# Cross-attention and FFN kernel: the two fp16 parts of a half of the probabilities turned by one transposing transfer instead of two

## The chip, the cores and the metric

The kernel runs on one core of one Trainium2 chip. The metric is the device time of one execution in microseconds (us). Engines are named as in the profile: PE is TensorE (PEld its weight loads), DVE is VectorE, ACT is ScalarE, POOL is GpSimd, and SP is SyncE, whose queue (SPq) issues nearly all the DMAs.

## What is computed

The inputs are `x` of 32 x 128 x 1024 and a context of 32 x 128 x 256, in float32. The reference, cut to what matters:

```python
def _layernorm(x):                      # over the last axis, eps 1e-5
    ...
def _L0_xattn_ref(pcd_up, pcd_down, Wq, Wk, Wv, Wskip):
    q = jnp.einsum('oc,bcn->bon', Wq, pcd_up)
    k = jnp.einsum('oc,bcm->bom', Wk, pcd_down)
    v = jnp.einsum('oc,bcm->bom', Wv, pcd_down)
    energy = jnp.einsum('bcn,bcm->bnm', q, k) / sqrt(C)
    attention = jax.nn.softmax(energy, axis=-1)
    return jnp.einsum('oc,bcn->bon', Wskip, pcd_up) + jnp.einsum('bnm,bcm->bcn', attention, v)
def _L0_ffn_ref(x, qweight, scales, zeros, bias):
    w = dequantised 4-bit weights, 1024 x 1024
    return jnp.einsum('bsi,io->bso', x, w) + bias
x = x + _L0_xattn_ref(_layernorm(x), ctx_1024, ...)
x = x + _L0_ffn_ref(_layernorm(x), ...)
```

## The kernel before, in words

One batch element b (128 channels by 1024 positions) is one unit of work; there are 32. The kernel is a software pipeline written out by hand: every engine has a function `step(t)`, and in step t it works on several elements at once: on n = t + 1 (centring, keys and values), b = t (scores and softmax), a = t - 1 (attention output, residual, second norm), q = t - 2 (the FFN) and c = t - 3 (output). There is no planner: each engine runs its calls in the order in which they are written, and semaphores tie the engines together. The first two steps have an order of their own (`run_in`).

Precision is held by splitting each float32 operand into a high and a low part. The probabilities of an element (1024 positions by 256 context columns) lie as 128 x 2048 in `prob`. They are handled in two halves h = 0 and 1 of 512 positions:

- POOL scales them by the inverse row sums (`normalise`, line 259), in four chunks j.
- ACT rounds a half to fp16, the high part (`probs_hi`, line 483, 128 x 1024 elements into `p_hi`).
- DVE takes the difference, the low part (`probs_lo`, line 662, into `p_lo`).
- SP turns both with transposing DMAs (`turn_probs`): line 166 for the high part once it is made, line 169 for the low part once that is made. Each moves 128 x 1024 fp16 elements from SBUF to SBUF. Both add 16 to `pt_loaded[h]`.
- PE waits for both (line 911) and multiplies with the values (`skip_attend`, line 914).

PE attends to half 0 of element a early in step t = a + 1 and to half 1 later in it. ACT writes `p_hi` of the next element only after the transfers of the last one have landed (line 482), and the new softmax overwrites `prob` only after the low part is made (line 472).

The normalised residual stream is turned in the same way: ACT makes `xn` and its high part (lines 492 and 501), POOL the low part (line 301), SP turns both (`turn_xn`, lines 177 and 183), and PE's `ffn` waits for both landings and runs 32 matmuls over them (line 919), with a closing matmul that adds the zero-point and bias terms (line 923).

SP's queue is strictly in order. In step t it issues: the two halves of an output (line 198), the next context and the next `x` (lines 147 and 144), `turn_probs(b, 0)`, `turn_probs(b, 1)`, `turn_xn(a)` and the three small copies of the row sums (line 189). Whatever one of these waits for, and however long its issue takes, holds up the ones behind it:

```python
if ran(b):
    turn_probs(b, 0)
    turn_probs(b, 1)
if ran(a):
    turn_xn(a)
```

The other places that the steps below touch: POOL computes the inverse standard deviation of the second norm (line 283) from DVE's variance (line 687), and from it the bias (line 285) that ACT needs for `xn`. DVE reads the maximum of the context from PSUM (line 615) as soon as PE's keys and values are done (line 897), adds the residual (line 672) and scales the FFN product (line 696).

Of the kernel before, what the change touches and what calls it, by code (L numbers as in the profile page):

```python
# [7 lines left out]
F16 = mybir.dt.float16  # L8
# [6 lines left out]
def xattn_ffn_program(nc, x, ctx_in, wq, wk, wv, wskip, qweight, scales, zeros, bias, out):  # L15
# [5 lines left out]
    P = nc.NUM_PARTITIONS  # L21
    HALF = 512
    HALVES = N // HALF
    NT = N // P
    MT = M // P
# [15 lines left out]
    with es:  # L41
        def sb(name, shape, dt=F32):
            return es.enter_context(nc.sbuf_tensor("sb_" + name, shape, dt))

        def pb(name, shape, dt=F32):
            return es.enter_context(nc.psum_tensor("ps_" + name, shape, dt))
# [4 lines left out]
        def sems(name, n):  # L51
            return [sem(f"{name}{k}") for k in range(n)]
# [30 lines left out]
        neg_max = sb("neg_max", [P, CHUNKS, TPC])  # L83
        esum = sb("esum", [P, CHUNKS, TPC])
        rsum = sb("rsum", [P, CHUNKS, TPC])
        p_hi, p_lo = (sb(n, [P, HALVES, MT, HALF], F16) for n in ("p_hi", "p_lo"))
        pt_hi, pt_lo = (sb(n, [P, HALVES, MT, HALF], F16) for n in ("pt_hi", "pt_lo"))
        x1 = sb("x1", [P, 3, N])
        xn = sb("xn", [P, KT, P])
        xn_hi, xn_lo = (sb(n, [P, KT, P], F16) for n in ("xn_hi", "xn_lo"))  # L90
        xnt_hi, xnt_lo = (sb(n, [P, 2, KT, P], F16) for n in ("xnt_hi", "xnt_lo"))
# [8 lines left out]
        ps_o = [pb(f"o{k}", [P, HALF]) for k in range(HALVES)]  # L100
# [19 lines left out]
        phi_done, plo_done, pt_loaded = sems("phi", HALVES), sems("plo", HALVES), sems("pt_loaded", HALVES)  # L120
# [8 lines left out]
        def ran(b, back=0):  # L129
            return 0 <= b - back < B  # L130
# [4 lines left out]
        def run_steps(step, first):  # L135
            for t in range(first, B + 3):
                step(t)
# [3 lines left out]
        @block.sync  # L141
        def _(sp):
            def load_x(k):
                sp.dma_start(x_sb[:, k % 4, :], x[k, :, :]).then_inc(x_loaded[k % 4], 16)

            def load_ctx(k):
                sp.dma_start(ctx_sb[:, k % 2, :], ctx_in[k, :, :]).then_inc(ctx_loaded[k % 2], 16)

            load_x(0)
            load_ctx(0)  # L150
            for dst, src in ((wv_sb, wv), (wskip_sb, wskip)):
                sp.dma_start(dst[:, :], src).then_inc(wvs_loaded, 16)
            q_tiles = qweight.rearrange("(t p) o -> p t o", p=P)
            load_x(1)
            load_ctx(1)
            for t in range(QT):
                sp.dma_start(q_sb[:, t, :], q_tiles[:, t, :]).then_inc(q_loaded[t], 16)
                if t == 1:
                    load_x(2)
            sp.dma_start(scale_row[:, :], scales.broadcast_to((P, OUT))).then_inc(row_loaded, 16)  # L160

            def turn_probs(b, h):
                sp.wait_ge(phi_done[h], b + 1)
                if ran(b, 1):
                    sp.wait_ge(attn_done[h], b)
                sp.dma_start_transpose(pt_hi[:, h, :, :].rearrange("m k (t n) -> m (k t) n", n=P),
                                       p_hi[:, h, :, :].rearrange("n k m -> n (k m)")).then_inc(pt_loaded[h], 16)
                sp.wait_ge(plo_done[h], b + 1)
                sp.dma_start_transpose(pt_lo[:, h, :, :].rearrange("m k (t n) -> m (k t) n", n=P),  # L169
                                       p_lo[:, h, :, :].rearrange("n k m -> n (k m)")).then_inc(pt_loaded[h], 16)  # L170

            def turn_xn(a):
                par = a % 2
                sp.wait_ge(xnhi_done, a + 1)
                if ran(a, 2):
                    sp.wait_ge(y_done[1], a - 1)
                sp.dma_start_transpose(xnt_hi[:, par, :, :],  # L177
                                       xn_hi[:, :, :].rearrange("c k r -> c (k r)")).then_inc(
                    last_hi_loaded if a == B - 1 else xnt_loaded[par], 16)
                sp.wait_ge(xnlo_done, a + 1)  # L180
                if a == B - 1:
                    sp.wait_ge(last_lo_done, 1)
                sp.dma_start_transpose(xnt_lo[:, par, :, :],
                                       xn_lo[:, :, :].rearrange("c k r -> c (k r)")).then_inc(xnt_loaded[par], 16)
                sp.wait_ge(rs3_done, a + 1)
                if a == 0:
                    sp.wait_ge(seed_made, 3)
                for k, row in ((0, 0), (1, 1), (0, 32)):
                    sp.dma_start(seed_l[row:row + 1, par, :].bitcast(F32),
                                 rs3[:, par, k:k + 1].bitcast(F32)).then_inc(rs_loaded[par], 16)  # L190

            def step(t):
                b, a, c = t, t - 1, t - 3
                if ran(c):
                    for h in range(HALVES):
                        cols = slice(h * HALF, (h + 1) * HALF)
                        sp.wait_ge(out_done[h], c + 1)
                        sp.dma_start(out[c, :, cols], o_sb[:, c % 2, cols]).then_inc(stored[c % 2], 16)
                if ran(t + 3):
                    sp.wait_ge(kv_done, t + 2)  # L200
                    load_ctx(t + 3)
                    sp.wait_ge(x1_done[1], a + 1)
                    load_x(t + 3)
# [6 lines that stand above are left out]
            def run_in():  # L210
                sp.wait_ge(kv_done, 1)
                load_ctx(2)
                load_x(3)
                turn_probs(0, 0)
                turn_probs(0, 1)
                sp.wait_ge(kv_done, 2)
                load_ctx(3)
                turn_probs(1, 0)
                sp.wait_ge(kv_done, 3)
                load_ctx(4)  # L220
                sp.wait_ge(x1_done[1], 1)
                load_x(4)
                turn_probs(1, 1)
                turn_xn(0)

            run_in()
            run_steps(step, 2)
            for par in range(2):
                sp.wait_ge(stored[par], 32 * (B // 2))
# [183 lines left out]
        def _(act):  # L413
# [64 lines left out]
            def probs_hi(b, h):  # L478
                act.wait_ge(norm_done[2 * h], b + 1)
                act.wait_ge(norm_done[2 * h + 1], b + 1)  # L480
                if ran(b, 1):
                    act.wait_ge(pt_loaded[h], 32 * b)
                act.activation(p_hi[:, h, :, :].rearrange("n k (t m) -> n k t m", m=P),  # L483
                               prob[:, 2 * h:2 * h + 2, :, :].rearrange("n j t (k m) -> n k (j t) m", m=P),
                               ACT.Copy).then_inc(phi_done[h], 1)

# [22 lines left out]
            def run_in():  # L509
# [8 lines left out]
                centred_hi(1)  # L518
                exps(0, 2)
                probs_hi(0, 0)  # L520
                exps(0, 3)
                keys_hi(1)
# [50 lines left out]
        def _(dve):  # L573
# [85 lines left out]

            def probs_lo(b, h):  # L660
                dve.wait_ge(phi_done[h], b + 1)
                dve.tensor_tensor(p_lo[:, h, :, :].rearrange("n k (t m) -> n k t m", m=P),  # L662
                                  prob[:, 2 * h:2 * h + 2, :, :].rearrange("n j t (k m) -> n k (j t) m", m=P),
                                  p_hi[:, h, :, :].rearrange("n k (t m) -> n k t m", m=P),
                                  ALU.subtract).then_inc(plo_done[h], 1)

            def residual(a, h):
# [185 lines left out]
        def _(pe):  # L853
            HI_LO = ((0, 0), (0, 1), (1, 0))
            wsk_p, xc_p, k_p, v_p = (wsk_hi, wsk_lo), (xc_hi, xc_lo), (k_hi, k_lo), (v_hi, v_lo)
            pt_p, xnt_p = (pt_hi, pt_lo), (xnt_hi, xnt_lo)

            pe.wait_ge(wkq_loaded, 32)
            pe.matmul(ps_o[0][:, 0:C], wk_sb[:, :], wq_sb[:, :], start=True, stop=True).then_inc(key_done, 1)
# [45 lines left out]
            def skip_attend(a, h):  # L905
                cols = slice(h * HALF, (h + 1) * HALF)
                if ran(a, 1):
                    pe.wait_ge(x1_done[h], a)
                for i, (s, m) in enumerate(HI_LO):
                    pe.matmul(ps_o[h][:, :], wsk_p[s][:, a % 3, :], xc_p[m][:, a % 3, cols], start=i == 0, stop=False)  # L910
                pe.wait_ge(pt_loaded[h], 32 * (a + 1))
                for k in range(MT):
                    for i, (s, m) in enumerate(HI_LO):
                        last = pe.matmul(ps_o[h][:, :], v_p[s][:, a % 3, k * P:(k + 1) * P], pt_p[m][:, h, k, :],  # L914
                                         start=False, stop=k == MT - 1 and i == 2)
                last.then_inc(attn_done[h], 1)

# [120 lines left out]
```

## Time and profile before

| | |
|---|---|
| runs of the kernel before | 530.37, 531.56 and 531.84 us, median 531.56 us |
| the profiled execution's own time | 532.22 us |
| its span, first to last instruction | 530.4 us |
| mean granted TensorE clock | 0.987 of full speed |

The profiled execution is one more run, 0.66 us above the median of the three. Durations below come from it. A line of a timeline gives the start (us from the start of the span) and the duration of an instruction or of a merged group (xN), then engine, line, operation and operands. A wait is idle time of an engine, put down to what ended it.

### The profile page before, as it was taken

How to read it: one execution, taken by the hardware profiler on the slowest of the kernel's cores; microseconds unless marked ns; L12 is line 12 of the kernel's file. 1: busy time of each engine (PE TensorE's matmuls, PEld its weight loads, DVE VectorE, ACT ScalarE, POOL GpSimd, SP SyncE). 2: the span in 40 equal slices, each digit the busy share in tenths (PEclk: the TensorE clock that was granted, in tenths of full speed). 3: DMA queues.
4: the chain of work that ended last, by engine and by line, in shares of the span. 5: the costliest groups of instructions: out<-in, count | busy, mean ns of one | idle time of the engine just before them, and what ended most of it. 6: DMA issues, size and time to landing. Idle time of an engine off the chain costs nothing.

```text
span 530.4 us, 9275 instructions
## 1 busy us (share of the span) xinstructions
PE 504.5 (95%) x2700; PEld 311.9 (59%) x2700; DVE 441.2 (83%) x982; ACT 369.7 (70%) x844; POOL 435.0 (82%) x649
## 2 busy tenths in 40 slices
PE   4659899999999999999999999999999999999987
PEld 3546565566666565666656566665656666565643
DVE  5899788899888889988888998888889888887752
ACT  4878876767787776777777677777767777777520
POOL 4888788898888889888888988888898888888753
PEclk9788999999999999999999999999999999999999
DMA  8727877788898799789888978987797889758864
GB/s 294 192 61 129 159 191 180 176 187 181 172 168 194 178 176 195 178 167 166 197 178 177 191 161 189 162 200 178 176 179 179 182 160 201 179 128 150 155 127 116
DMA packets 236787, 91.65 MB, mean 173 GB/s; under 512 B 219200, under 2 KB 223808, under 8 KB 236736
## 3 DMA queue, kind: packets, MB, share of 16 engines
q1 hardware_dynamic: 236016, 90.92, 79.8%
q8 instruction: 21, 0.34, 0.3%
q14 instruction: 30, 0.25, 0.2%
q10 hardware_dynamic: 720, 0.14, 0.1%
HBM read 23.87 MB, written 16.78 MB: 77 GB/s over the span
## 4 chain that ended last, share of the span: by engine, by line
POOL 63%; issue 14%; ACT 7%; PE 3%; DVE 1%; DMA 1%; SPq 1%; POOLq 0%; ACTq 0%
POOL sb_prob L259 13%; POOL sb_xc_lo L274 13%; POOL sb_xn_lo L301 13%; POOL sb_o L253 12%; ACT sb_xn L492 6%; POOL sb_nb L285 4%; POOL sb_rstd L283 3%; PE ps_y L919 3%; POOL sb_rstd L267 3%; POOL sb_rs L293 1%; POOL sb_rs L295 1%; DMA sb_xnt_lo<-sb_xn_lo 1%; ACT sb_xn_hi L501 0%; SPq L169 0%; SPq L177 0%
## 5 line engine op out<-in xcount | busy, mean ns | idle before, releaser
L919 PE MATMUL ps_y<-sb_wf,sb_xnt_hi 128*128 128x512 f16 x512 | 192.3, 380 | 3.6 <-ACT sb_wf L506 1.9
L919 PE MATMUL ps_y<-sb_wf,sb_xnt_lo 128*128 128x512 f16 x512 | 191.8, 379 | 0.0
L474 ACT ACTIVATE sb_prob<-ps_e,sb_neg_max 128x256 f32<-128x256 f32 x256 | 118.0, 469 | 35.8 <-DVE sb_neg_max L653 35.7
L259 POOL TENSOR_SCALAR sb_prob<-sb_prob,sb_rsum 128x256 f32<-128x256 f32 x256 | 123.2, 497 | 4.1 <-DVE sb_rsum L658 4.1
L662 DVE TENSOR_TENSOR sb_p_lo<-sb_prob,sb_p_hi 128x1024 f16<-128x1024 f32 x64 | 78.1, 1220 | 49.3 <-ACT sb_p_hi L483 49.3
L301 POOL TENSOR_TENSOR sb_xn_lo<-sb_xn,sb_xn_hi 128x512 f16<-128x512 f32 x63 | 75.2, 1214 | 44.2 <-ACT sb_xn_hi L501 44.2
L483 ACT ACTIVATE sb_p_hi<-sb_prob 128x1024 f16<-128x1024 f32 x64 | 67.3, 1051 | 51.4 <-issue 47.5
L884 PE MATMUL ps_e<-sb_k_hi,sb_xc_hi 128*128 128x256 f32 x256 | 85.1, 332 | 10.3 <-DVE sb_k_lo L641 5.5
L919 PEld LDWEIGHTS ps_y<-sb_wf,sb_xnt_hi 128*128 128x128 f16 x512 | 49.9, 98 | 67.7 <-issue 8.3
L653 DVE TENSOR_REDUCE sb_neg_max<-ps_e 128x2 f32<-128x512 f32 x128 | 84.6, 679 | 1.3 <-PE ps_e L884 1.2
L253 POOL TENSOR_TENSOR sb_o<-sb_prod,sb_x 128x512 f32<-128x512 f32 x63 | 80.3, 1295 | 5.4 <-DVE sb_prod L696 5.4
L919 PEld LDWEIGHTS ps_y<-sb_wf,sb_xnt_lo 128*128 128x128 f16 x512 | 50.1, 98 | 53.0 <-issue 0.5
L274 POOL TENSOR_TENSOR sb_xc_lo<-sb_xc,sb_xc_hi 128x512 fp32r<-128x512 f32 x62 | 80.4, 1296 | 0.0
L492 ACT ACTIVATE sb_xn<-sb_x,sb_nb,sb_rstd 128x1024 f32<-128x1024 f32 x32 | 42.9, 1340 | 51.4 <-POOL sb_nb L285 51.4
L884 PE MATMUL ps_e<-sb_k_lo,sb_xc_hi 128*128 128x256 f32 x256 | 73.6, 287 | 0.0
L884 PE MATMUL ps_e<-sb_k_hi,sb_xc_lo 128*128 128x256 f32 x256 | 73.5, 287 | 0.0
L884 PEld LDWEIGHTS ps_e<-sb_k_hi,sb_xc_hi 128*128 128x128 f32 x256 | 49.9, 195 | 20.2 <-DVE sb_k_lo L641 11.2
L696 DVE TENSOR_TENSOR sb_prod<-ps_y,sb_scale_row 128x512 f32<-128x512 f32 x64 | 43.6, 681 | 11.5 <-PE ps_y L923 11.5
L884 PEld LDWEIGHTS ps_e<-sb_k_lo,sb_xc_hi 128*128 128x128 f32 x256 | 50.0, 195 | 2.7
L474 ACT ACTIVATION_READ_ACCUMULATOR sb_prob<-ps_e,sb_neg_max 128x1 f32 x256 | 51.0, 199 | 0.0
L672 DVE SCALAR_TENSOR_TENSOR sb_x<-ps_o,sb_o_scale,sb_x 128x512 f32<-128x512 f32 x64 | 47.2, 738 | 3.8 <-PE ps_o L914 3.8
L914 PE MATMUL ps_o<-sb_pt_hi,sb_v_hi 128*128 128x512 f16 x128 | 49.7, 388 | 0.7 <-DMA sb_pt_lo<-sb_p_lo 0.7
(115 smaller groups left out, 936.9 us busy)
## 6 DMA issues: line engine op xcount, KB each, us to landing
sb_x<-in_x_dram SPq DMA_DIRECT2D x32, 512.0 KB, 4.2
out_dram<-sb_o SPq DMA_DIRECT2D x64, 256.0 KB, 2.5
sb_ctx<-in_ctx_dram SPq DMA_DIRECT2D x32, 128.0 KB, 2.9
sb_q<-in_L_ffn_qweight_dram SPq DMA_DIRECT2D x4, 512.0 KB, 9.7
sb_seed_l<-sb_rs SPq DMA_DIRECT2D x96, 0.5 KB, 2.2
sb_pt_hi<-sb_p_hi SPq DMA_TRANSPOSE x64, 4.2
sb_pt_lo<-sb_p_lo SPq DMA_TRANSPOSE x64, 3.4
sb_scale_row<-in_L_ffn_scales_dram SPq DMA_DIRECT2D x1, 512.0 KB, 10.7
```

The lines of the kernel that those rows point to most:

```text
L253: pool.tensor_tensor(o_sb[:, c % 2, cols], prod[:, h, :], x1[:, c % 3, cols], ALU.add).then_inc(out_done[h], 1)
L259: last = pool.tensor_scalar(prob[:, j, t, :], prob[:, j, t, :], rsum[:, j, t:t + 1], P_SCALE, ALU.mult, ALU.mult)
L274: last = pool.tensor_tensor(xc_lo[:, n % 3, cols], xc[:, cols], xc_hi[:, n % 3, cols].bitcast(F32), ALU.subtract)
L301: last = pool.tensor_tensor(xn_lo[:, k:k + KT // 2, :], xn[:, k:k + KT // 2, :], xn_hi[:, k:k + KT // 2, :], ALU.subtract)
L474: done = act.activation(prob[:, j, t, :], ps_e[j % 2][:, t, :], ACT.Exp, bias=neg_max[:, j, t:t + 1], accum_out=esum[:, j, t:t + 1])
L483: act.activation(p_hi[:, h, :, :].rearrange("n k (t m) -> n k t m", m=P), prob[:, 2 * h:2 * h + 2, :, :].rearrange("n j t (k m) -> n k (j ...
L492: act.activation(xn[:, :, :].rearrange("c (t e) r -> c t e r", e=2), x1[:, a % 3, :].rearrange("c (t r e) -> c t e r", e=2, r=P), ACT.Iden ...
L653: dve.tensor_reduce(neg_max[:, j, :], ps_e[j % 2][:, :, :], AX.X, ALU.max, negate=True).then_inc(max_done[j], 1)
L662: dve.tensor_tensor(p_lo[:, h, :, :].rearrange("n k (t m) -> n k t m", m=P), prob[:, 2 * h:2 * h + 2, :, :].rearrange("n j t (k m) -> n k ...
L884: last = pe.matmul(ps_e[j % 2][:, t, :], xc_p[s][:, b % 3, cols], k_p[m][:, b % 2, :], start=i == 0, stop=i == 2)
L914: last = pe.matmul(ps_o[h][:, :], v_p[s][:, a % 3, k * P:(k + 1) * P], pt_p[m][:, h, k, :], start=False, stop=k == MT - 1 and i == 2)
L919: pe.matmul(ps_y[h][:, :], xnt_p[s][:, q % 2, kt, :], wf[:, kt, h * HALF:(h + 1) * HALF], start=kt == 0 and s == 0, stop=False)
```

## The change

The four tiles `p_hi`, `p_lo`, `pt_hi` and `pt_lo` become two, `p_parts` and `pt_parts`, in which the high part (index 0) and the low part (index 1) of each half lie side by side in a partition. `probs_hi` and `probs_lo` write into their part of `p_parts`. `turn_probs` waits for both parts, and then issues one transposing transfer of 128 x 2048 elements where there were two of 128 x 1024. A half's semaphore `pt_loaded[h]` therefore grows by 16 for each element instead of 32, and the waits for it are changed to match. The bytes moved, the instructions of ACT and DVE and the matmuls stay as they are.

```diff
-        p_hi, p_lo = (sb(n, [P, HALVES, MT, HALF], F16) for n in ("p_hi", "p_lo"))
-        pt_hi, pt_lo = (sb(n, [P, HALVES, MT, HALF], F16) for n in ("pt_hi", "pt_lo"))
+        p_parts = sb("p_parts", [P, HALVES, 2, MT, HALF], F16)
+        pt_parts = sb("pt_parts", [P, HALVES, 2, MT, HALF], F16)
...
                 sp.wait_ge(phi_done[h], b + 1)
                 if ran(b, 1):
                     sp.wait_ge(attn_done[h], b)
-                sp.dma_start_transpose(pt_hi[:, h, :, :].rearrange("m k (t n) -> m (k t) n", n=P),
-                                       p_hi[:, h, :, :].rearrange("n k m -> n (k m)")).then_inc(pt_loaded[h], 16)
                 sp.wait_ge(plo_done[h], b + 1)
-                sp.dma_start_transpose(pt_lo[:, h, :, :].rearrange("m k (t n) -> m (k t) n", n=P),
-                                       p_lo[:, h, :, :].rearrange("n k m -> n (k m)")).then_inc(pt_loaded[h], 16)
+                sp.dma_start_transpose(pt_parts[:, h, :, :, :].rearrange("m s k (t n) -> m (s k t) n", n=P),
+                                       p_parts[:, h, :, :, :].rearrange("n s k m -> n (s k m)")).then_inc(pt_loaded[h], 16)
...
                 if ran(b, 1):
-                    act.wait_ge(pt_loaded[h], 32 * b)
-                act.activation(p_hi[:, h, :, :].rearrange("n k (t m) -> n k t m", m=P),
+                    act.wait_ge(pt_loaded[h], 16 * b)
+                act.activation(p_parts[:, h, 0, :, :].rearrange("n k (t m) -> n k t m", m=P),
...
-                dve.tensor_tensor(p_lo[:, h, :, :].rearrange("n k (t m) -> n k t m", m=P),
+                dve.tensor_tensor(p_parts[:, h, 1, :, :].rearrange("n k (t m) -> n k t m", m=P),
...
-                pe.wait_ge(pt_loaded[h], 32 * (a + 1))
+                pe.wait_ge(pt_loaded[h], 16 * (a + 1))
                 for k in range(MT):
                     for i, (s, m) in enumerate(HI_LO):
-                        last = pe.matmul(ps_o[h][:, :], v_p[s][:, a % 3, k * P:(k + 1) * P], pt_p[m][:, h, k, :],
+                        last = pe.matmul(ps_o[h][:, :], v_p[s][:, a % 3, k * P:(k + 1) * P], pt_parts[:, h, m, k, :],
```

## Rows read from the trace of the kernel before

**Rows 1.** The page, part 1: busy time of each engine.
```profile
PE 504.5 (95%) x2700; PEld 311.9 (59%) x2700; DVE 441.2 (83%) x982; ACT 369.7 (70%) x844; POOL 435.0 (82%) x649
```

**Rows 2.** The page, part 4: the chain that ended last, by engine.
```profile
POOL 63%; issue 14%; ACT 7%; PE 3%; DVE 1%; DMA 1%; SPq 1%; POOLq 0%; ACTq 0%
```

**Rows 3.** Timeline of POOL over one step: start, duration, line.
```profile
260.33 2.38 POOL L301 TENSOR_TENSOR sb_xn_lo<-sb_xn,sb_xn_hi 128x512 f16<-128x512 f32 x2 [1.44 <-ACT sb_xn_hi L501]
...
270.93 0.56 POOL L283 TENSOR_TENSOR sb_rstd<-sb_ve,sb_neg_half 128x1 f32<-128x1 f32 x1
...
275.77 2.38 POOL L301 TENSOR_TENSOR sb_xn_lo<-sb_xn,sb_xn_hi 128x512 f16<-128x512 f32 x2 [1.44 <-ACT sb_xn_hi L501]
```

**Rows 4.** Timeline of PE around two steps, the instructions that wait for DMAs.
```profile
251.99 0.39 PE L919 MATMUL ps_y<-sb_wf,sb_xnt_hi 128*128 128x512 f16 x1
...
260.75 0.61 PE L897 MATMUL ps_kv<-sb_proj,sb_ctx 128*128 128x128 f32 x4
...
261.89 0.39 PE L914 MATMUL ps_o<-sb_pt_hi,sb_v_hi 128*128 128x512 f16 x1
...
265.33 0.39 PE L914 MATMUL ps_o<-sb_pt_hi,sb_v_hi 128*128 128x512 f16 x1
...
267.36 0.39 PE L919 MATMUL ps_y<-sb_wf,sb_xnt_hi 128*128 128x512 f16 x1
```

**Rows 5.** Waits of PE's weight loads, 100 to 500 us: total us, times, longest.
```profile
PEld ps_y L919 <- DMA sb_xnt_lo<-sb_xn_lo: 1.2, 4, 0.5
PEld ps_o L914 <- DMA sb_pt_lo<-sb_p_lo: 1.0, 2, 0.7
```

**Rows 6.** Timeline of SP's queue, 248 to 270 us: start and duration of each issue.
```profile
248.66 1.36 SPq L183 DMA_TRANSPOSE sb_xnt_lo<-sb_xn_lo  x1
...
256.79 1.23 SPq L169 DMA_TRANSPOSE sb_pt_lo<-sb_p_lo  x1
259.33 1.23 SPq L166 DMA_TRANSPOSE sb_pt_hi<-sb_p_hi  x1
260.60 1.34 SPq L169 DMA_TRANSPOSE sb_pt_lo<-sb_p_lo  x1
262.04 1.28 SPq L177 DMA_TRANSPOSE sb_xnt_hi<-sb_xn_hi  x1
263.36 1.34 SPq L183 DMA_TRANSPOSE sb_xnt_lo<-sb_xn_lo  x1
264.75 1.89 SPq L189 DMA_DIRECT2D sb_seed_l<-sb_rs  x3
266.68 1.06 SPq L198 DMA_DIRECT2D out_dram<-sb_o  x2
```

**Rows 7.** Four transfers by line, windows 247:255, 256:258, 260:262, 262:275: issue to landing.
```profile
L183 SPq DMA_TRANSPOSE sb_xnt_lo<-sb_xn_lo x1: 1363/1363/1363, 248.7 to 248.7; - x1
...
DMA to landing us min/median/max: 3.3/3.3/3.3
...
L169 SPq DMA_TRANSPOSE sb_pt_lo<-sb_p_lo x1: 1233/1233/1233, 256.8 to 256.8; - x1
...
DMA to landing us min/median/max: 3.1/3.1/3.1
...
L169 SPq DMA_TRANSPOSE sb_pt_lo<-sb_p_lo x1: 1336/1336/1336, 260.6 to 260.6; - x1
...
DMA to landing us min/median/max: 3.4/3.4/3.4
...
L183 SPq DMA_TRANSPOSE sb_xnt_lo<-sb_xn_lo x1: 1342/1342/1342, 263.4 to 263.4; - x1
...
DMA to landing us min/median/max: 3.2/3.2/3.2
```

**Rows 8.** Short windows: busy time of each engine, then clock, DMA share and GB/s.
```profile
259.50:260.45 0.95, 0.95 (x10) 0.95 (x9) 0.95 (x1) 0.95 (x2) 0.12 (x1) 1.00 0.00 0
260.50:261.90 1.40, 1.40 (x10) 1.03 (x9) 1.36 (x5) 0.89 (x2) 1.40 (x2) 1.00 0.99 189
...
267.10:267.70 0.60, 0.60 (x6) 0.41 (x5) 0.60 (x1) 0.14 (x2) 0.60 (x1) 1.00 0.13 1
267.80:268.80 1.00, 1.00 (x6) 0.49 (x5) 1.00 (x4) 0.00 (x0) 1.00 (x3) 1.00 1.01 373
```

**Rows 9.** Timeline of DVE in the same step: the instructions tied to PE and POOL.
```profile
261.68 0.15 DVE L615 TENSOR_SCALAR sb_t_scale<-ps_m 128x1 f32<-128x1 f32 x1
...
270.62 0.15 DVE L687 TENSOR_SCALAR sb_ve<-sb_mv 128x1 f32<-128x1 f32 x1
```

**Rows 10.** The chain that ended last, in order of time, 504 to 515 us.
```profile
504.09 1.24 DVE sb_p_lo L662
505.32 0.04 issue
505.36 1.39 SPq L169
...
506.85 1.28 SPq L177
508.13 0.04 issue
508.18 3.20 DMA sb_xnt_lo<-sb_xn_lo
511.38 0.05 issue
511.43 3.63 PE ps_y L919 x16
```

More of the change, by code:

```diff
@@ L661, in probs_lo @@
                 dve.wait_ge(phi_done[h], b + 1)
-                dve.tensor_tensor(p_lo[:, h, :, :].rearrange("n k (t m) -> n k t m", m=P),
+                dve.tensor_tensor(p_parts[:, h, 1, :, :].rearrange("n k (t m) -> n k t m", m=P),
                                   prob[:, 2 * h:2 * h + 2, :, :].rearrange("n j t (k m) -> n k (j t) m", m=P),
-                                  p_hi[:, h, :, :].rearrange("n k (t m) -> n k t m", m=P),
+                                  p_parts[:, h, 0, :, :].rearrange("n k (t m) -> n k t m", m=P),
                                   ALU.subtract).then_inc(plo_done[h], 1)
@@ L855, in _ @@
             wsk_p, xc_p, k_p, v_p = (wsk_hi, wsk_lo), (xc_hi, xc_lo), (k_hi, k_lo), (v_hi, v_lo)
-            pt_p, xnt_p = (pt_hi, pt_lo), (xnt_hi, xnt_lo)
+            xnt_p = (xnt_hi, xnt_lo)
             pe.wait_ge(wkq_loaded, 32)
```

## The prediction, made before the changed kernel was run

> **What bounds the kernel now.** I read the page first, then the chain that ended last, the waits of each engine, and a timeline of one step. By busy time PE looks like the bound, at 95% [rows 1]. But the chain of work that ended last lies 63% on POOL and 3% on PE [rows 2]. The timeline tells how both can be. POOL's `xn_lo` of one step starts at 260.33 and of the next at 275.77, a period of 15.44 us, and POOL waits in it only for work that ACT does on POOL's own results [rows 3]. PE's first FFN matmul starts at 251.99 and again at 267.36, a period of 15.37 [rows 4]. So two loops run side by side, POOL's being 0.07 us a step slower. PE creeps forward against POOL until it meets a transfer that isn't there yet: in the 400 us from 100 to 500, some 26 steps, it waited 4 times for the turned `xn_lo` and 2 times for the turned `p_lo`, 2.2 us in all [rows 5]. These waits cost nothing today, since POOL sets the pace. What counts is how much later a landing may come before the delay travels through PE and DVE into POOL.
>
> **The slack of each landing.** For one ordinary step, issue [rows 6] plus issue to landing [rows 7] against the matmul that needs it [rows 4]:
> - Half 0: issued 256.79, + 3.1 = 259.9, needed 261.89, slack 2.0.
> - Half 1: 260.60 + 3.4 = 264.0, needed 265.33, slack 1.3.
> - `xn_lo`: 263.36 + 3.2 = 266.6, needed 267.36, slack 0.8.
> - `xn_lo` one step earlier, a late one: 248.66 + 3.3 = 251.96, needed 251.99, slack 0.03.
>
> Behind PE there is a little more. PE's keys and values end at 260.75 + 0.61 = 261.36 [rows 4] and DVE reads them at 261.68, 0.32 later; DVE's variance is ready at 270.77 [rows 9] and POOL takes it at 270.93 [rows 3], 0.16 later. Between the two I see DVE without idle time. So a landing of `xn_lo` may come later by 0.8 + 0.32 + 0.16 = 1.3 us in an ordinary step and by 0.03 + 0.48 = 0.5 in a late one. Anything beyond goes into POOL's loop, and so into the time.
>
> **The change, part by part.** *Removed:* 64 issues of 1.23 us on SP (line 166). *Kept:* the bytes; ACT's and DVE's instructions have the same shapes and counts, so I cost them at nothing. *Changed:* each half's transfer is now issued when the low part is made (256.79, 260.60), and is twice as long. The high part loses its head start of 2.5 us in half 0 and 1.3 in half 1.
>
> What a double transfer costs isn't in the trace. Bounds for its issue: not under one issue, 1.23 us; two issues back to back, 1.23 + 1.34 = 2.6 [rows 6]. I take 2.4, near the upper end, because the data side is as slow as the issue side: with the first transfer issued at 259.33, no byte moves from 259.50 to 260.45, and from 260.50 on the DMA engines are 0.99 busy at 189 GB/s [rows 8]. One part is 128 x 1024 x 2 = 0.26 MB, which at 189 to 211 GB/s is 1.2 to 1.4 us; a gap-free stream of two parts saves at most a tenth or two. (211 is 0.26 MB over one 1.24 us issue.)
>
> Does the stream start while the double transfer is still being issued? The plain DMAs of the outputs help: issue of two from 266.68 to 267.74, no data until 267.70, and 373 GB/s from 267.80 [rows 8]. There the data come 1.1 us after the first issue begins, and that issue takes about half of 1.06 us [rows 6], so data lag the end of an issue by some 0.5 us. For a transposing one they begin at its end or just before. So its first pieces must have been handed over half way through, and a double one should start to move at + 1.2 too. Its landing is then later than that of the second of two transfers by the time of one part less what overlapped.
>
> - Half 0: 3.1 + 1.2 = 4.3 us after 256.79, at 261.1; slack 2.0 goes to 0.8. Costs nothing; if late, it would be PE's first attention matmul.
> - Half 1: before, `p_lo` queued just behind `p_hi`. Now 260.60 + 3.4 + 1.0 = 265.0; slack 1.3 goes to 0.3. In the two waits for `p_lo` of rows 5 it goes under zero by 1.0, but PE's next FFN waits then anyway.
> - `turn_xn`, moved behind a longer issue: before, SP was free at 260.60 + 1.34 = 261.94, now at 260.60 + 2.4 = 263.0. The issues of lines 177 and 183 move from 262.04 and 263.36 to 263.05 and 264.4, so both land 1.0 us later, `xn_lo` at 267.6. PE now waits 0.2 to 0.3 us in an ordinary step.
> - Behind it on SP stand the three row-sum copies, the outputs, the next context and `x`, all + 1.0. The row sums were issued at 264.75, and their matmul comes after 16 FFN matmuls; I cost them at nothing, and if that cover went, line 923 would wait.
>
> **The sum.** An ordinary step has 1.3 us of slack against 1.0: nothing. A late step has 0.5 against 1.0: 0.5 us each. How many are late? Rows 5 record 6 waits in 26 steps; the one at 251.99 isn't among them as a long wait, and with such near misses I estimate 8 to 9, so 10 in the 30 steps that turn an `xn` behind probabilities. That gives 10 x 0.5 = 5.0 us. At the end there is no slack: the chain goes from DVE's last `p_lo` through SP's issue at 505.36 (1.39 us) and line 177 to the `xn_lo` transfer and the last FFNs [rows 10]; 1.0 us more. Sum: 6.0 us. On the profiled execution's own 532.22 that is 538.2; the median of the runs shown is 0.66 lower, so I say 537.6.
>
> The unknown is the lateness D of `xn_lo`, 1.0 here. With D = 0.5 late steps cost nothing, and the sum is 0.5; with D = 1.3 they cost 0.8 each, ordinary ones begin to count, and the sum is about 10.
>
> The trace has one part in 1.2 to 1.4 us. The Trainium skill (DMA: Bandwidth & Descriptors, "Latency and other measured facts") gives 261 GB/s for a transposing DMA as measured; by that an estimate for the double transfer is 2.0 us, D would be about 0.5, and the time 532.1. The same page's rule to coalesce transfers ("Rules for kernel authors") speaks for the change, but no transfer here is of the small kind that it means.
>
> **The rivals.**
> *A. Not slower: one long transfer streams better.* If the double issue takes no more than 1.34 + 0.5 = 1.84 us, `xn_lo` comes at most 0.5 late and the slack takes it. Time 532.1, within the noise. For it: every issue has some fixed part, and SP issues of plain DMAs take only some 0.5 us each. Against: the DMA engines are full while a part moves [rows 8], and a faster issue doesn't help a full engine. If even the single issue's length held, nothing would be gained beyond PE's idle waits, as POOL paces the loop.
> *B. Transfer only after the whole issue.* If data move only once all is issued, the first byte comes at + 2.4 instead of + 1.2, half 1 lands 1.2 later still, and `xn_lo` queues behind it: D = 2.1. Late steps then cost 2.1 - 0.5 = 1.6 each, ordinary ones 0.8, though the path from FFN back to the next but one `xn_lo` takes two steps, so about 5 of those count: 16 + 4 + 2 = 22 us, 554. For it: in rows 8 the data of a single transfer start about when its issue ends. Against: the half microsecond of lag in the plain DMAs.
> *C. The transfer is cut into two again by whatever expands it.* Then both parts are issued back to back after the low part, 2.6 us of issue, D = 1.1 to 1.2: 540. It is the upper end of my own case.
>
> **How the numbers follow.** A difference under 0.3% (1.6 us) can't be told from no change here. My forecast with C has 0.68, from 533.5 to 542; A 0.17; B 0.11; a remaining 0.04 for a gain that I have no mechanism for. Slower is 0.80, same 0.16 (most of A), faster 0.04. The range, 531 to 545, holds my case and A, with the late steps counted up to 14, and leaves out B and the gain.
>
> **What would show it.** Right: the issue of the merged transfer takes 2.2 to 2.6 us and lands 4.2 to 4.6 after it starts; SP's line for `xnt_lo` starts 1.0 later against POOL's step; PE's waits for `xnt_lo` grow from 1.2 us to 5 or more in the same window; POOL's wait for DVE's variance, absent now, appears in some steps; a few steps are longer than 15.44. Wrong: the issue under 1.9 us (A), landing over 5 us (B), or waits on PE that grow while POOL's period stays: then the slack behind PE was larger than the 0.48 I read.

## The result, and the profile after

The changed kernel takes 534.04 us (median of 6 runs, 533.51 to 535.31), the kernel before 531.46 (6 runs, 530.37 to 531.87). The ratio is 1.0052, with a 95% interval of 1.0038 to 1.0066: slower by 2.6 us, where I forecast 6.0. The direction is right, the time is inside the range, and the size is less than half of the forecast. The profiled execution has a span of 533.5 us, 3.1 more than before. It is the slowest of its six runs (535.31 us), so the 3.1 holds some scatter from run to run. The granted clock isn't the cause: it is 1.00 from 100 to 500 us in both traces.

The page of the changed kernel, parts 1 and 4, against [rows 1, 2]:

```profile
PE 504.7 (95%) x2700; PEld 311.8 (58%) x2700; DVE 430.4 (81%) x982; ACT 370.5 (69%) x844; POOL 435.0 (82%) x649
...
POOL 38%; PE 15%; issue 11%; DVE 10%; ACT 6%; DMA 6%; SPq 4%; POOLq 0%; ACTq 0%
```

POOL's share of the chain fell from 63% to 38%, and DMA, PE, DVE and SP came in: the chain now crosses from transfers into POOL in some steps. The other change is easily missed. DVE is busy 10.8 us less than before, with the same 982 instructions. Where that comes from is shown below; it is the key to the size of the loss.

SP's queue in an ordinary step, against [rows 6] (start, duration):

```profile
262.35 1.97 SPq L175 DMA_TRANSPOSE sb_xnt_hi<-sb_xn_hi  x1
264.37 1.33 SPq L181 DMA_TRANSPOSE sb_xnt_lo<-sb_xn_lo  x1
```

and the two merged transfers of the same step, by line, in windows 256:258 and 260:262, against [rows 7]:

```profile
L167 SPq DMA_TRANSPOSE sb_pt_parts<-sb_p_parts x1: 1808/1808/1808, 256.8 to 256.8; - x1
...
DMA to landing us min/median/max: 4.3/4.3/4.3
...
L167 SPq DMA_TRANSPOSE sb_pt_parts<-sb_p_parts x1: 1673/1673/1673, 260.6 to 260.6; - x1
...
DMA to landing us min/median/max: 4.3/4.3/4.3
```

The landing of the merged transfer came out as worked out, 4.3 us after its issue. Its issue did not: 1.7 to 1.8 us in this step (median of all 64: 1.9) instead of 2.4. Yet `xn_lo` is issued at 264.37 where it was 263.36, 1.0 us later, just as forecast. The time that the merged issue saved appears in the next one: line 175 now takes 1.97 us where line 177 took 1.28 [rows 6]. Two short windows of the same step (busy times of the engines, then clock, DMA share and GB/s) tell what the data did:

```profile
260.70:261.70 1.00, 1.00 (x9) 0.95 (x9) 0.98 (x2) 0.53 (x1) 1.00 (x2) 1.00 0.00 0
261.80:264.80 3.00, 3.00 (x20) 2.07 (x19) 2.48 (x11) 2.87 (x8) 3.00 (x3) 1.00 1.10 210
```

The merged transfer is issued at 260.58 and its issue lasts until 262.25, but data move from about 261.8 on, so it streams while it is issued. From there the DMA engines are full, at 210 GB/s, through the merged transfer and into the next one. Before, the stream was as full, but it began at 260.50 [rows 8], with the high part. So `xn` comes 1.0 us later because the stream starts that much later. That fits the DMA engines, and not the length of an issue on SP, as what sets the pace here; no run varied the length of an issue by itself.

PE's waits for DMAs between 100 and 500 us, against [rows 5], and POOL's waits for DVE in the same window (total us, times, longest):

```profile
PEld ps_o L912 <- DMA sb_pt_parts<-sb_p_parts: 3.4, 7, 0.9
PEld ps_y L917 <- DMA sb_xnt_lo<-sb_xn_lo: 2.4, 6, 0.6
POOL sb_prob L257 <- DVE sb_rsum L656: 1.9, 7, 0.5
```

PE's weight loads wait 5.8 us now against 2.2, and POOL, which never waited for DVE before in this window, does so 7 times. That is the new wait through which the loss enters POOL's loop. It stands at line 257 (`normalise`), for the inverse row sums, and not at the inverse standard deviation where I expected it.

**Where the 3.1 us of span come from.** I took the start of POOL's `xn_lo` for each element from the timelines of both kernels. Up to element 2 the changed kernel is 0.5 us ahead. That isn't an effect of the change: over the ten traces of this case this start lies anywhere from 73.6 to 75.4 us. From element 2 to element 28 (26 periods) the kernel before takes 401.6 us and the changed one 403.4: + 1.8. From there to the end it is 53.9 before and 55.6 after: + 1.7. Before, all 26 periods are 15.43 to 15.46 us. After, 21 are 15.40 to 15.50 us, and five are longer: 15.78, 15.76, 15.82, 16.36 and 15.78, which is 2.2 us above 15.45 in all; the ordinary periods, 0.02 to 0.03 shorter than before, give 0.4 back.

### The profile page after: what moved, and what is told of

It is laid out like the page before. It is cut to its first block, busy times and chain, and to the rows that moved or that the text cites. A ratio compares the mean times of both kernels' runs of the same rounds, so it can differ in the third digit from the quotient of the medians.

```text
span 533.5 us, 9213 instructions
## 1 busy us (share of the span) xinstructions
PE 504.7 (95%) x2700; PEld 311.8 (58%) x2700; DVE 430.4 (81%) x982; ACT 370.5 (69%) x844; POOL 435.0 (82%) x649
## 4 chain that ended last, share of the span: by engine, by line
POOL 38%; PE 15%; issue 11%; DVE 10%; ACT 6%; DMA 6%; SPq 4%; POOLq 0%; ACTq 0%
PE ps_y L917 11%; POOL sb_prob L257 8%; POOL sb_xc_lo L272 8%; POOL sb_xn_lo L299 8%; POOL sb_o L251 6%; ACT sb_xn L490 5%; DMA sb_xnt_lo<-sb_xn_lo 3%; POOL sb_nb L283 3%; DMA sb_pt_parts<-sb_p_parts 2%; POOL sb_rstd L281 2%; SPq L175 2%; SPq L167 2%; POOL sb_rstd L265 2%; DVE sb_p_parts L660 2%; DVE sb_x L670 1%
## 5 line engine op out<-in xcount | busy, mean ns | idle before, releaser
L660 DVE TENSOR_TENSOR sb_p_parts<-sb_prob,sb_p_parts 128x1024 f16<-128x1024 f32 x64 | 78.1, 1220 | 46.3 <-ACT sb_p_parts L481 46.3
L481 ACT ACTIVATE sb_p_parts<-sb_prob 128x1024 f16<-128x1024 f32 x64 | 67.2, 1050 | 30.2 <-issue 26.4
L912 PE MATMUL ps_o<-sb_pt_parts,sb_v_hi 128*128 128x512 f16 x256 | 76.9, 382 | 2.6 <-DMA sb_pt_parts<-sb_p_parts 2.6
```

Source lines behind the costliest of these rows:

```text
L481: act.activation(p_parts[:, h, 0, :, :].rearrange("n k (t m) -> n k t m", m=P), prob[:, 2 * h:2 * h + 2, :, :].rearrange("n j t (k m) -> n ...
L660: dve.tensor_tensor(p_parts[:, h, 1, :, :].rearrange("n k (t m) -> n k t m", m=P), prob[:, 2 * h:2 * h + 2, :, :].rearrange("n j t (k m) - ...
```

## The longest step, row by row

The period of 16.36 us is the one to read. SP's queue in it, from the changed kernel's timeline:

```profile
338.07 1.94 SPq L167 DMA_TRANSPOSE sb_pt_parts<-sb_p_parts  x1
340.10 2.49 SPq L175 DMA_TRANSPOSE sb_xnt_hi<-sb_xn_hi  x1
342.64 1.34 SPq L181 DMA_TRANSPOSE sb_xnt_lo<-sb_xn_lo  x1
```

PE and then DVE, from the same timeline (in brackets the idle time before an instruction and what ended it):

```profile
344.40 0.60 PE L912 MATMUL ps_o<-sb_pt_parts,sb_v_hi 128*128 128x512 f16 x2 [0.46 <-DMA sb_pt_parts<-sb_p_parts]
...
346.95 0.39 PE L917 MATMUL ps_y<-sb_wf,sb_xnt_hi 128*128 128x512 f16 x1 [0.37 <-DMA sb_xnt_lo<-sb_xn_lo]
...
354.55 0.69 DVE L694 TENSOR_TENSOR sb_prod<-ps_y,sb_scale_row 128x512 f32<-128x512 f32 x1 [1.06 <-PE ps_y L921]
...
356.36 0.16 DVE L613 TENSOR_SCALAR sb_t_scale<-ps_m 128x1 f32<-128x1 f32 x1 [0.41 <-PE ps_kv L895]
```

POOL, from one `xn_lo` to the next:

```profile
353.24 2.38 POOL L299 TENSOR_TENSOR sb_xn_lo<-sb_xn,sb_xn_hi 128x512 f16<-128x512 f32 x2 [1.44 <-ACT sb_xn_hi L499]
...
358.64 0.93 POOL L257 TENSOR_SCALAR sb_prob<-sb_prob,sb_rsum 128x256 f32<-128x256 f32 x2 [0.54 <-DVE sb_rsum L656]
...
362.52 0.93 POOL L257 TENSOR_SCALAR sb_prob<-sb_prob,sb_rsum 128x256 f32<-128x256 f32 x2 [0.22 <-DVE sb_rsum L656]
...
369.61 2.38 POOL L299 TENSOR_TENSOR sb_xn_lo<-sb_xn,sb_xn_hi 128x512 f16<-128x512 f32 x2 [1.45 <-ACT sb_xn_hi L499]
```

The merged transfer of half 1 is issued at 338.07 and lands 6.3 us later in place of 4.3 (its "DMA to landing"), PE waits for it and then for `xn_lo`, the FFN starts at 346.95, DVE waits 1.06 us for its product and 0.41 for the keys and values, and POOL waits 0.54 and 0.22 us for row sums. So both waits of PE, for half 1 and for `xn_lo`, stand in the same step; the last one is for `xn_lo`, which queues behind the merged transfer.

**Where the slack behind PE was.** DVE's instruction that makes the low part of the skip weights (`wsk_lo`, line 646 before, 644 after), grouped by line from 100 to 500 us: before, then after.

```profile
L646 DVE SCALAR_TENSOR_TENSOR sb_wsk_lo<-sb_proj,sb_sk_scale,sb_wsk_hi 128x128 fp32r<-128x128 f32 x25 | 29.0, 1162 | 0.0
```

```profile
L644 DVE SCALAR_TENSOR_TENSOR sb_wsk_lo<-sb_proj,sb_sk_scale,sb_wsk_hi 128x128 fp32r<-128x128 f32 x25 | 11.9, 476 | 0.0
```

The same instruction on the same shape takes 1162 ns in one kernel and 476 in the other. In the step shown next its start moved from 266.84 to 267.48, and its end hardly at all. Both ends lie 0.15 us behind the end of a POOL instruction with which it shares no data:

```profile
266.84 1.19 DVE L646 SCALAR_TENSOR_TENSOR sb_wsk_lo<-sb_proj,sb_sk_scale,sb_wsk_hi 128x128 fp32r<-128x128 f32 x1
...
266.59 1.29 POOL L274 TENSOR_TENSOR sb_xc_lo<-sb_xc,sb_xc_hi 128x512 fp32r<-128x512 f32 x1
```

```profile
267.48 0.46 DVE L644 SCALAR_TENSOR_TENSOR sb_wsk_lo<-sb_proj,sb_sk_scale,sb_wsk_hi 128x128 fp32r<-128x128 f32 x1
...
266.52 1.26 POOL L272 TENSOR_TENSOR sb_xc_lo<-sb_xc,sb_xc_hi 128x512 fp32r<-128x512 f32 x1
```

That isn't one step alone: in both kernels, and in the runs below that leave the instruction where it is, its end lies 0.14 to 0.15 us behind the end of a POOL instruction in most steps, while its duration has medians from 0.42 to 1.18 us. So most of the 1162 ns is a wait. The timeline counts this wait as busy time, with no releaser. DVE may start 0.7 us later and still finish at the same time. This is the slack that I missed: 0.32 + 0.16 = 0.48 us behind PE in the prediction, about 1.1 in fact.

## The experiments

**One half at a time.** `MERGED` names the halves that use the merged transfer; the other keeps two transfers, in the same tiles, and its semaphore counts 32.

```diff
+                if h in MERGED:
+                    sp.wait_ge(plo_done[h], b + 1)
+                    sp.dma_start_transpose(pt_parts[:, h, :, :, :]..., p_parts[:, h, :, :, :]...).then_inc(pt_loaded[h], 16)
+                    return
+                for s in range(2):
+                    if s == 1 or h in LATE:
+                        sp.wait_ge(plo_done[h], b + 1)
+                    sp.dma_start_transpose(pt_parts[:, h, s, :, :]..., p_parts[:, h, s, :, :]...).then_inc(pt_loaded[h], 16)
```

Half 0 alone:

> Only half 0 is merged; half 1 keeps its two transfers. Theory S (the cost sits in the late landings of half 1 and in the last steps, where xn_lo queues behind it): half 0 has 2.0 us of slack and loses 1.2, so nothing happens, the time is that of the kernel before within 0.3% (530.5 to 532.5), and PE's waits for the turned probabilities stay near 1.0 us between 100 and 500 us. Rival M (a merged transfer costs by itself, wherever it stands): about half of the loss, 532.5 to 533.

Measured: 531.31 us against 531.39, ratio 1.000 (0.999 to 1.0009). Half 0 costs nothing, and neither does the new layout of the tiles. PE's waits for probabilities were 1.6 us, not 1.0, and cost nothing either:

```profile
PEld ps_o L921 <- DMA sb_pt_parts<-sb_p_parts: 1.6, 4, 0.8
```

Half 1 alone:

> Only half 1 is merged. Theory S: nearly the whole loss of the full change, 533.5 to 534.3. Rival M: about half of it, 532.5 to 533. In both xn_lo is issued 1.0 to 1.1 us later against POOL's step.

Measured: 533.81 us, ratio 1.0042 (1.0026 to 1.0057), and `xn_lo` is issued 1.05 us later against POOL's step, as expected. Half 1 carries the loss. It is the half whose transfer stands directly ahead of those of `xn` on SP's queue.

**Two transfers, both issued late** (`MERGED` empty, `LATE` both halves):

> Two transfers in each half as before, but both are issued only once the low part is made. If the lost head start is the cost (theory S), this loses as much as the change or a little more: 533.5 to 535. If the length of one transfer is the cost (rival M), it is close to the kernel before: 531 to 532.5.

Measured: 536.42 us, ratio 1.010 (1.0084 to 1.0116): 5.0 us lost, more than expected, twice the loss of the change. So it is the lost head start that costs; once it is given up, one transfer is better than two. Against POOL's `xn_lo`, the low `xn` transfer lands at 6.4 us in the kernel before (median of the timelines' issues plus their landings), 7.5 with the merged transfer and 7.7 here. Only 0.25 us lie between the last two, but nine periods instead of five came out over 15.5 us.

**Only `xn` late.** The kernel before, with small DMAs put on SP's queue between the two kinds of transfer, in every step that has both. The probabilities are issued as before.

```diff
                 if ran(a):
+                    if ran(b):
+                        for k in range(2):
+                            sp.dma_start(spare[t:t + 1, k, :], wk_sb[0:1, :]).then_inc(spare_done, 16)
                     turn_xn(a)
```

> The kernel before with two small DMAs of 512 B put on SP's queue between the probabilities' transfers and those of xn, which start about 1.2 us later; the probabilities land as before. Theory of the prediction (slack behind PE is 0.48 us, late steps cost 0.5 each or more): 536 to 539. Theory S (DVE's step holds more slack, 0.7 us of it inside the 1.16 us instruction on line 646, so a late xn_lo is absorbed except at the end): 532 to 533.3, with POOL's period unchanged at 15.4 in nearly all steps.

Measured: 539.04 us, ratio 1.0142 (1.0125 to 1.0158), 7.6 us lost. At first sight this is my prediction's theory and not the new one. The trace says otherwise: POOL's 26 periods sum to only 2.7 us more than before, six of them over 15.5. The delay was also larger than planned, 1.65 us (median) instead of 1.2, since the queue stayed full from step to step; in about ten steps the low part of half 1 was issued later too, by 0.1 to 1.0 us. And 4.4 us were lost after element 28, where DVE makes the second half of the last `xn` low part only after it has scaled an FFN product, for which it waited 6.3 us here (the line below); SP can't issue that transfer before. So this end isn't comparable with the changed kernel's, and the run doesn't price a late `xn` by itself. The time lies outside the ranges of both theories. The run does show that a late `xn` alone produces POOL's new wait: from 100 to 500 us PE never waits for half 1, and POOL waits for DVE 9 times.

```profile
522.92 0.69 DVE L702 TENSOR_TENSOR sb_prod<-ps_y,sb_scale_row 128x512 f32<-128x512 f32 x1 [6.28 <-PE ps_y L929]
...
POOL sb_prob L265 <- DVE sb_rsum L664: 2.3, 9, 0.4
```

With one small DMA in place of two:

> The kernel before with one small DMA (0.6 us of SP's queue) ahead of the transfers of xn, in place of two. The law of a threshold (nothing until the FFN starts 8.1 to 8.2 us after POOL's xn_lo, then one for one): at most one or two steps longer than 15.5 us, and the loss is 0.5 to 1.5 us, most of it at the end: 532 to 533. A loss in proportion to the delay (half of the 7.6 us that two of them cost) gives 535.

Measured: 533.02 us against 531.27, ratio 1.0031 (1.0021 to 1.0042), just above what was expected. The `xn` transfer lands 0.7 us later than before, and only one period of the 26 is over 15.5 (15.52). In the trace the 26 periods take 0.7 us less than before and the end after element 28 takes 1.1 more, so this loss sits at the end. A delay of 0.7 costs 1.75 us, one of 1.65 costs 7.6 with the end in it: not in proportion.

**The law behind these runs.** I took it from the changed kernel and the first four runs; the one with a single small DMA and the three that follow the table were its tests. For each step I took the start of PE's first FFN matmul, counted from the start of POOL's `xn_lo` of the same element, and POOL's period that follows it. The latest ones, leaving out steps right after a longer one (there POOL has moved along already, and the same lateness costs nothing again):

| run | FFN start, us after `xn_lo` | POOL's period that follows |
|---|---|---|
| before | 7.57 | 15.44 |
| half 0 merged | 8.12 | 15.44 |
| one small DMA | 8.21 / 8.26 | 15.52 / 15.50 |
| changed kernel | 8.34 / 8.39 / 8.44 / 8.60 / 9.20 | 15.78 / 15.76 / 15.78 / 15.82 / 16.36 |
| half 1 merged | 8.26 / 8.58 | 15.54 / 15.81 |
| two transfers, both late | 8.63 / 8.93 / 9.05 | 15.86 / 16.17 / 16.29 |
| two small DMAs | 8.59 / 8.86 / 8.93 | 15.84 / 16.12 / 16.17 |
| `wsk_lo` moved, changed kernel | 8.54 / 8.70 | 15.56 / 15.72 |

Up to 8.1 or 8.2 us nothing happens, with one step as an exception (8.07 and 15.56 with half 1 merged; in the same step 15.50 and 15.51 in two other runs, which I can't explain); beyond it the period grows by roughly the excess. In the longest step above it is 346.95 - 337.75 = 9.20, and 16.36 - 15.45 = 0.91.

**The hidden wait taken out.** DVE's `wsk_lo` moved out of `values_lo` to a place just ahead of the second probabilities' low part, where DVE idles for ACT anyway and POOL waits too:

```diff
             def values_lo(n):
                 dve.wait_ge(kvhi_done, n + 1)
-                dve.scalar_tensor_tensor(wsk_lo[:, n % 3, :], ...)
+                if n < 3:
+                    skip_lo(n)
...
+                if ran(n):
+                    skip_lo(n)
                 if ran(b):
                     probs_lo(b, 1)
```

In the changed kernel:

> The changed kernel with DVE's low part of the skip weights (the 128 x 128 instruction that took 1.16 us before and 0.48 after) moved to the end of DVE's step, ahead of the second probabilities' low part, where DVE and POOL both wait for ACT. Theory R (that instruction holds a hidden wait for POOL, and with it the slack that took up most of the late transfers; steps grow only when the FFN's first matmul starts over 8.1 to 8.2 us after POOL's xn_lo): the instruction takes under 0.35 us in its new place, the threshold rises by the 0.4 us that it no longer takes in the chain, so the five longer steps shrink to one or two, and the time falls by 1 to 2 us, to 532 to 533; the loss at the end stays. If the slack was elsewhere: no change, 534.

Measured: 532.62 us against 531.27, ratio 1.0018 (1.0009 to 1.0027). How much of that is the slack is told by the same move in the kernel before, below. The instruction in its new place:

```profile
L643 DVE SCALAR_TENSOR_TENSOR sb_wsk_lo<-sb_proj,sb_sk_scale,sb_wsk_hi 128x128 fp32r<-128x128 f32 x26 | 8.9, 343 | 0.0
```

343 ns, as expected, and in most steps no POOL instruction runs beside it there; so 0.8 of the 1.16 us were waiting. The threshold rose (table: 8.54 gives 15.56, where 8.44 gave 15.78 before the move), though by less than the 0.4 us expected: after a late step the FFN's start settles at 8.35 us, where it settled at 8.09 in the changed kernel; and the longer periods shrank from 0.3 to 0.9 us over 15.45 to at most 0.3. There are four of them, where I expected one or two. The ordinary period fell as well, to 15.38, which is PE's own pace [rows 4].

In the kernel before:

> The kernel before with the same move. Theory R: no transfer is late enough to matter here, so only POOL's ordinary period can change, from 15.44 to about 15.41 us as in the changed kernel, where DVE's instruction did not wait: 530.3 to 531.4. If the move itself costs: above 532.

Measured: 531.05 us, ratio 0.9991 (0.9982 to 0.9999). The ordinary period is 15.39, 0.05 less. This is the run to hold the last one against, since the move shortens ordinary periods by itself: with the instruction moved in both, the change costs 1.6 us (532.62 against 531.05; 1.4 by the two ratios), where it costs 2.6 without the move. So a good two fifths of the loss are gone. The traces place the gain in the steps: from element 2 to 28 the change costs 0.6 us with the move (400.3 and 400.9) in place of 1.8, and after element 28 it costs 1.8 as before. That is what more slack behind PE should do, as the end has none. The move also takes the instruction itself out of the chain, so it doesn't price the hidden wait alone.

With half 0 merged too:

> Only half 0 merged, plus the same move: a candidate to beat both. Theory R: as the kernel before with the move, 530 to 531.3.

Measured: 530.89 us, ratio 0.9993 (0.9984 to 1.0002). Both are ahead of the changed kernel by 3 us, and by 0.2 and 0.4 us of the kernel before, which is less than a measurement of this kernel can tell.

## Why the prediction was right in sign and wrong in size

- *The reading of the bound* held: POOL's loop sets the pace, and a landing matters only when it gets through PE and DVE into it.
- *The cost of the double transfer* was right in its result and partly by luck. Landing after 4.3 us in both halves, and `xn_lo` issued 1.0 us later and landing at 267.6, are as forecast. But I derived the 1.0 from an issue of 2.4 us, and the issue took 1.7 to 1.8 here; what came 1.0 later was the start of a full stream. Rival A was bound to an issue under 1.84 us. 23 of the 64 issues met that, without `xn` coming any earlier; its against ("a faster issue doesn't help a full engine") was the true part.
- *Streaming*: the double transfer starts to move while it is issued, as the lag of the plain DMAs told. Rival B (D = 2.1) is out. Rival C is out too: there is one issue per half. The Trainium skill (DMA: Bandwidth & Descriptors, "Latency and other measured facts") gives 261 GB/s for a transposing DMA with a non-contiguous middle dimension, and 350 to 400 for a contiguous one. By the 261, D would have been 0.5; the trace has 210 GB/s and 1.0, so the measurement decides, and the page's figures don't hold here.
- *Half 0 costs nothing*: confirmed by its own run. *Half 1*: it did meet waits in late steps, and in the longest step they fell together with those of `xn`, as I said.
- *The number of late steps*, 10, was good: in the kernel before, `xn_lo` landed less than 0.15 us ahead of the FFN's start in 10 of 30 steps. What I had wrong is that each of them costs.
- *The step that failed* is the slack behind PE: "Between the two I see DVE without idle time", and so 0.32 + 0.16 us, and 0.5 us of cost in each of 10 late steps, 5.0 us. DVE had no idle time, but it had 0.7 us of waiting inside an instruction of 128 x 128 elements that took 1.16 us. The room can be read from the law: in the late step that I worked with, the FFN started 7.10 us after `xn_lo` (251.99 - 244.89), and it may start at 8.1 to 8.2, so there is 1.0 to 1.1 us of room and not 0.5. With D = 1.0 such a step costs nothing, and that is what most late steps did. Five steps did cost, 2.2 us together, less 0.4 for the shorter ordinary ones: 1.8 in place of 5.0. In those five `xn_lo` landed 1.0 to 2.0 us later than in the kernel before, so a single D for all steps was a simplification too, and it hid part of the first error.
- *The gate* was another one, POOL's `normalise` instead of line 283.
- *The ordinary step* was misread as well. I expected PE to wait 0.2 to 0.3 us there. In the step shown `xn_lo` landed at 267.6 as forecast, and PE came for it at 268.27 without a wait: late steps had pushed PE back, and its pace regains only some 0.05 us a step.
- *The end* was undersized: 1.0 forecast, 1.7 measured after element 28. The last chain was priced well: from the start of DVE's last low part to the landing of `xn_lo` it takes 7.29 us before [rows 10] and 8.25 after. What I left out are the two periods before it, which POOL doesn't pace any more (15.27 and 13.99 us, before 14.91 and 13.62):

```profile
506.12 1.24 DVE sb_p_parts L660
...
507.43 2.01 SPq L167
...
509.53 1.63 SPq L175
511.16 0.05 issue
511.22 3.16 DMA sb_xnt_lo<-sb_xn_lo
```

Sum: - 0.5 + 1.8 + 1.7 = 3.0, against a span that grew by 3.1.

Of the signs that I had named as right, three came (the landing, `xn_lo` 1.0 later, a few longer steps) and three didn't: the issue of 2.2 to 2.6 us, PE's waits for `xnt_lo` of 5 us or more (2.4 measured), and POOL's wait for the variance. Of those named as wrong, an issue under 1.9 us (A) was met in nearly half of the transfers, and a landing over 5 us (B) in 11 of the 32 of half 1, neither with the result of its rival. The last one came in most steps: PE waits more while POOL's period stays, "then the slack behind PE was larger than the 0.48 I read".

## What to carry to other kernels

Merging two transfers saves an issue but gives up the head start of the first; before doing it, find what queues behind the merged one, since that is what comes late (here `xn`, not the probabilities). Slack must be read from both ends of a chain. An instruction that takes far longer than its neighbours on a shape no larger (here 1.16 us beside 0.47), on an engine "without idle time", may hold a wait. And a delay within the slack costs nothing, while what goes beyond it costs nearly in full, so a loss shouldn't be scaled from one experiment to another. Last, a helper edit needs its own control: moving `wsk_lo` shortened the ordinary periods of both kernels.

## What I hadn't expected of the hardware

**DVE and POOL.** A DVE instruction with both tensor operands in SBUF took 1162, 476 or 343 ns (means) on one shape, depending on how much of POOL's neighbouring instruction it overlapped. That it waits for something the two engines share fits all three numbers; which resource it is was not tried.

**Late transfers and instruction loading.** Of the 12 merged transfers of half 1 that landed late, 10 had a 16 KB packet of instruction loading start while they were under way, one had two packets of 8 KB, and the twelfth was issued 1.1 us after one of 16 KB; none of the 20 ordinary ones had a 16 KB packet. Landing late is nothing new: in the kernel before, 13 low parts of half 1 took 3.7 us or more in place of 3.3 to 3.4, and 11 of them had such a packet. In the longest step, the DMA view from 337.5 to 345 us shows one, and a stretch at 7 to 10 GB/s in the middle of the transfer:

```profile
GB/s 180 223 111 0 0 0 0 0 0 85 217 218 199 209 302 209 177 38 0 0 0 7 8 10 10 168 292 289 291 308 272 281 37 8 8 26 284 288 274 291
...
q8 instruction: 1, 0.02, 1.0%
```

So the transposing transfer comes nearly to a halt at about the time of one 16 KB packet, for about 1.2 us here. It is a correlation in the traces; no run removed the instruction loads. Two merged transfers of half 0 also landed late (5.1 and 5.2 us) without a 16 KB packet, so it isn't the only cause.
